# Three batches' experts issued eleven slots later in a one-core transformer kernel

## The chip, the cores and the metric

The kernel runs on one core of a Trainium2 chip. The metric is the device time of one execution in microseconds (us), the median of three runs. The core has five engines that run side by side, each working through its own queue in order: TensorE (PE, matmuls into PSUM; its weight loads are listed as PEld), VectorE (DVE), ScalarE (ACT, activation functions), GpSimd (POOL) and SyncE (SP, which here issues the DMAs). They meet only through semaphores.

## The reference

The input is four batches of 512 tokens with 128 channels. Four blocks follow each other, each added to the stream through a layer norm, `x = x + _layernorm(block(_layernorm(x)))`:

```
1  six layers of banded attention (16 heads of 8, a query sees 125 keys back and itself), each with a
   feed-forward part of 512 hidden channels and two layer norms
2  a mixer: r * ((relu(k) ** 2) @ W_v), with r and k from the token and the one before it
3  causal attention, 16 heads of 8; a gate that depends on the key's phase scales the weights
4  experts:
     pooled = x.mean(axis=1)
     h = jnp.tanh(pooled @ W1 + b1)
     probs = jax.nn.softmax(h @ W2 + b2)
     top_p, top_i = jax.lax.top_k(probs, 3)
     w = top_p / top_p.sum()
     x + sum over the three chosen e of w[e] * gelu(x @ Wa[e]) @ Wb[e]      (hidden size 512, of 8 experts)
```

Which experts a batch uses is known only when its stream has passed block 3, and the expert's weights are fetched by that number.

## The kernel before

All work is cut into units. The six banded layers of four batches are 24 units (`UNITS`), the causal attention of the four batches another four. Each unit has a fixed timetable in slots, and `whole_phase` walks through all slots `g` once for every engine: in each slot it asks small functions (`maxima_due`, `exps_due`, `late_due`, `experts_due`, ...) what is due, and issues it in the order in which the questions stand. So the program of every engine is fixed by these numbers alone, and units overlap because their timetables do: `base(u)` is 8 + 16 u for a banded unit, and 402, 422, 442, 462 for the causal attention of batch 0 to 3.

```
QP, KP = 0, 1
MAX0 = 8
EXP0 = 23
TAIL = (EXP0 + 16, EXP0 + 22)
CAT, OUT = 2, 3
ROUTE = TAIL[1] + OUT + 7
EXPERT0 = ROUTE + 5
ENDING = EXPERT0 + 2 * TOP + 1
```

For the causal attention of a batch, counted from its base: projections in slots 0 and 1; maxima of the scores in 8 to 27 (PE `causal_maxima`, L479, then DVE `maxima`, L1005); scores again, exponentials and weighted sums in 23 to 44 (PE `scores`, L511, ACT `exponent`, L802, PE `weighted`, L530); transposes of the sums at 45 (L601), of the heads at 47 (L610), the output projection at 48 (`project_out`, L622). Then comes a chain that crosses all engines: the norm of the block's output at 49 and the norm of the new stream at 52 (`statistics` on DVE, L1140 and L1144; `norm_root` on POOL, L1363 to L1370; `scale_norm` on ACT, L890; `norm_add` on POOL, L1375), transposed rows (`turn_rows` on PE, L662, `place_rows` on ACT, L898), the router at 55 (L694, L911), its logits at 56 (L702, L1187), the exponential (L916) and the choice at 57 (`route_top`, L1194 to L1201), and at 58 the loads of the three experts' weights by SP (`load_expert`, L1509 and L1511) and the spreading of their shares (L711, L1205).

The experts stand at 60, 62 and 64: `expert_hidden` (PE, L719, four chunks of 512 columns) with `expert_gelu` (ACT, L925, four gelus); two slots after each, at 62, 64 and 66, `expert_out` (PE, L730, 32 matmuls in the trace) with `add_expert` (DVE, L1210). At 67 (`ENDING`) the last norm of the batch begins, at 69 its part of the output is stored (L1547).

Three things tie the engines together there. PE writes scores and expert chunks into the same three PSUM banks (`a`), each of which must be emptied by ACT before its next use, and maxima, projections and expert outputs into four banks (`d`) that DVE empties. ACT changes its function table (ACT_TABLE_LOAD, 1.28 us in the trace) between exponentials and gelus. And the expert weights have four buffers, so that a load for job n waits until job n - 4 has been through `expert_out`.

Since the bases are 20 slots apart, batch b's experts fall into the maxima, exponentials and transposes of batch b + 1 and the first maxima of batch b + 2. Batch 0 has its experts in slots 462 to 468, batch 1 in 482 to 488, batch 2 in 502 to 508, batch 3 in 522 to 528. The output projections are in slots 450, 470, 490 and 510.

Of the kernel before, what the change touches and what calls it, by code (L numbers as in the profile page):

```python
# [6 lines left out]
BATCH, SEQ = 4, 512  # L7
# [6 lines left out]
EXPERTS, ROUTER, TOP = 8, 32, 3  # L14
# [25 lines left out]
UNITS = LAYERS * BATCH  # L40
# [30 lines left out]
TAIL = (EXP0 + 16, EXP0 + 22)  # L71
CAT, OUT = 2, 3
# [5 lines left out]
ROUTE = TAIL[1] + OUT + 7  # L78
EXPERT0 = ROUTE + 5
ENDING = EXPERT0 + 2 * TOP + 1  # L80

COL_BQ, COL_BK, COL_BV, COL_G1, COL_H1, COL_G2, COL_H2, COL_B1 = range(8)
COLS = 7 + CHUNKS
# [24 lines left out]
def base(u):  # L108
    return BASE + SLOTS * u if u < UNITS else CAUSAL0 + CSLOTS * (u - UNITS)
# [6 lines left out]
def due(g, at, late=None):  # L116

    late = at if late is None else late
    return [u for u in range(ALL) if base(u) + (late if causal(u) else at) == g]
# [50 lines left out]
def norm_slot(b, k):  # L170


    last = base(UNITS - BATCH + b) + AFTER
    late = base(UNITS + b)
    return (SLOTS * b, SLOTS * b + 2, last, last + 3, last + MIX + 3, last + MIX + 6,
            late + TAIL[1] + OUT + 1, late + TAIL[1] + OUT + 4, late + ENDING)[k]


def norms_due(g, at=0):
    return [(b, k) for k in range(9) for b in range(BATCH) if norm_slot(b, k) + at == g]  # L180


def turns_due(g):
    return [(b, k) for k in (1, 3, 5, 7) for b in range(BATCH) if norm_slot(b, k) + (3 if k == 1 else 2) == g]
# [7 lines left out]
def late_due(g, at):  # L192

    return [b for b in range(BATCH) if base(UNITS + b) + at == g]


def experts_due(g, at):
    return [(b, r) for b in range(BATCH) for r in range(TOP) if base(UNITS + b) + EXPERT0 + 2 * r + at == g]


def loads_due(g):
    return [l for l in range(2, LAYERS + 1) if base((l - 1) * BATCH) + SLOTS * BATCH - 6 == g]


TOTAL = base(ALL - 1) + ENDING + 3

# [10 lines left out]
def whole_phase(nc, env):  # L217

    D, A, N, S = Turns(4), Turns(3), Turns(), Turns()
    for g in range(TOTAL):  # L220
# [50 lines left out]
        for b, r in experts_due(g, 0):  # L271
            for f in range(CHUNKS):
                A.add("ehid", b, r, f)
        for b, r in experts_due(g, 2):
            D.add("eout", b, r)
# [5 lines left out]
    with ExitStack() as ctx:  # L281
# [125 lines left out]
        def tokens(t):  # L407
            return t.rearrange("p (i c) -> p i c", c=P)
# [12 lines left out]
        def _(pe):  # L421
# [313 lines left out]
            for g in range(TOTAL):  # L735
# [52 lines left out]
                for b, r in experts_due(g, 0):  # L788
                    expert_hidden(b, r)
# [190 lines left out]
        def _(dve):  # L980
# [275 lines left out]
            for g in range(TOTAL):  # L1256
# [32 lines left out]
                for b in range(BATCH):  # L1289
                    if g == norm_slot(b, 1) + 2:  # L1290
                        place(b)
# [166 lines left out]
        def _(sp):  # L1458
            d = env["dram"]

            def load(l):
                par = l % 2
                if l >= 2:
                    sp.wait_ge(xres_ready, 2 * BATCH * (l - 1))
                    sp.wait_ge(a_emptied, A.n("norm", BATCH * (l - 1) - 1, 1))
                sp.dma_start(wqk[:, par, :], d["wqk"][l]).then_inc(w_loaded[par], 16)
                sp.dma_start(cols[:, par, :], d["cols"][l]).then_inc(w_loaded[par], 16)
                sp.dma_start(wv[:, par, :], d["wv"][l]).then_inc(w_loaded[par], 16)
                sp.dma_start(wo[:, par, :], d["wo"][l]).then_inc(w_loaded[par], 16)
                if l < LAYERS:  # L1470
                    sp.dma_start(rowt[:, par, :, :].rearrange("p n c -> p (n c)"), d["rowt"][l]
                                 ).then_inc(w_loaded[par], 16)
                    sp.dma_start(w1[:, par, :], d["w1"][l]).then_inc(w_loaded[par], 16)
                    sp.dma_start(w2[:, par, :, :].rearrange("p f c -> p (f c)"), d["w2"][l]).then_inc(w_loaded[par], 16)
# [6 lines left out]
            def pack(u, name):  # L1481
                roles = QROLES if name == "q" else KROLES
                parts_, lo, packed = (qparts, q_lo, q_packed) if name == "q" else (kparts, k_lo, k_packed)
                if u >= BUFS:
                    sp.wait_ge(a_filled, A.n("exp", u - BUFS, PAIRS - 1, banks_of(u - BUFS) - 1))
                else:
                    sp.wait_ge(q_clean if name == "q" else k_clean, u + 1)
                sp.wait_ge(lo, u + 1)
                for r, n in enumerate(roles):
                    dest = (qpack[r:P:ROLE_STEP, u % BUFS, 1:1 + PAIRS * SEQ] if name == "q"  # L1490
                            else kpack[r:P:ROLE_STEP, u % BUFS, :, 0:HEADED])
                    sp.dma_start(dest, parts_[:, n, :]).then_inc(packed, 16)

            def load_max(u, half):
                sp.wait_ge(a_emptied, A.n("parts", u, half))
                for part in range(PARTS):
                    for h in range(2):
                        first = 1 + (2 * h + half) * 2 * SEQ
                        sp.dma_start(qpack[BODY + part:P:64, u % BUFS, first:first + 2 * SEQ],
                                     mrows[:, part * P + 64 * h:part * P + 64 * h + 64]).then_inc(max_loaded, 16)  # L1500

            def load_expert(b, r):
                n = job(b, r)
                if n >= EBUFS:
                    sp.wait_ge(d_filled, D.n("eout", (n - EBUFS) // TOP, (n - EBUFS) % TOP))
                elif n >= 2:
                    sp.wait_ge(d_filled, D.n("ffn", UNITS - 1))
                e = sp.value_load(number[0:1, b, r:r + 1], min_val=0, max_val=EXPERTS - 1)
                sp.dma_start(w1[:, (n + 2) % EBUFS, :], d["wa"][bass.ds(e, 1)].rearrange("o p c -> (o p) c")  # L1509
                             ).then_inc(e_loaded[n % EBUFS], 16)  # L1510
                sp.dma_start(w2[:, (n + 2) % EBUFS, :, :].rearrange("p f c -> p (f c)"),  # L1511
                             d["wb"][bass.ds(e, 1)].rearrange("o p c -> (o p) c")).then_inc(e_loaded[n % EBUFS], 16)
# [18 lines left out]
            for g in range(TOTAL):  # L1531
                for half in range(2):
                    for u in due(g, MAX0 + 10 + 8 * half, MAX0 + 12 + 10 * half):
                        load_max(u, half)
                for u in due(g, QP + 1):
                    pack(u, "q")
                for u in due(g, KP + 1):
                    pack(u, "k")
                for l in loads_due(g):
                    load(l)  # L1540
                for b in late_due(g, ROUTE + 3):
                    sp.wait_ge(chosen_ready, b + 1)
                    for r in range(TOP):
                        load_expert(b, r)
                for b in late_due(g, ENDING + 2):
                    sp.wait_ge(added, S.n(b, 8))
                    sp.dma_start(env["out_rows"][:, b * TILES:(b + 1) * TILES, :], tokens(stream[:, b, :])  # L1547
                                 ).then_inc(stored, 16)
# [93 lines left out]
```

## Time and profile before

| | us |
|---|---|
| median of three runs | 1324.84 (1324.23 to 1325.89) |
| the profiled execution, its own time | 1324.06 |
| its span, first to last instruction | 1322.3 |
| PE busy | 1049.7 |
| DVE busy | 801.6 |
| ACT busy | 779.2 |
| POOL busy | 404.7 |
| mean granted clock of TensorE | 0.916 of full speed |

The time of an execution is some 1.8 us longer than its span. Busy times count instructions that compute; an engine that waits for a semaphore is not busy. A row of the timeline gives the start and length in us, the engine, the line of the kernel, the operation and, in brackets, the idle time before it and what ended it. The granted clock (PEclk) is 1.00 at 2.4 GHz and 0.50 at 1.2 GHz; values in between are a mean over a stretch.

### The profile page before, as it was taken

The numbers are of one execution on the slowest core, as the hardware profiler recorded it, in microseconds if no ns is written. First come the engines' busy times: TensorE is split into PE (matmuls) and PEld (weight loads), VectorE is DVE, ScalarE is ACT, GpSimd is POOL, SyncE is SP. The second block draws the span as 40 slices with busy tenths as digits, with TensorE's granted clock in tenths as the row PEclk, the third lists the DMA queues.
The fourth block names the chain that finished last, engine by engine and source line by source line (L and its number), as shares of the span: only waits on it lengthen the run. The fifth ranks groups of instructions, "written<-read, shape, count | busy, mean of one in ns | idle before, by whom it ended". The sixth has DMA issues, their size and how long they took to land.

```text
span 1322.3 us, 46954 instructions
## 1 busy us (share of the span) xinstructions
PE 1049.7 (79%) x20080; PEld 725.7 (55%) x20080; DVE 801.6 (61%) x2451; ACT 779.2 (59%) x1419; POOL 404.7 (31%) x544
## 2 busy tenths in 40 slices
PE   1466999999999999988999899977667768887935
PEld 0245666666666666666666666655434335444513
DVE  2466667666666777775666766666477765643111
ACT  5144666666666666656666666665545757566531
POOL 4323233332323323322233333334444422202020
PEclk9578999999999999999999999989768979897957
DMA  4211212213211311131221321200201203010110
GB/s 133 48 51 51 50 52 51 52 51 87 51 37 44 85 46 46 41 85 51 51 52 51 87 52 51 52 11 16 36 14 37 42 12 97 11 50 9 49 56 9
DMA packets 72626, 64.79 MB, mean 49 GB/s; under 512 B 16226, under 2 KB 66914, under 8 KB 72418
## 3 DMA queue, kind: packets, MB, share of 16 engines
q1 hardware_dynamic: 72418, 61.78, 18.4%
q8 instruction: 159, 2.61, 0.8%
q14 instruction: 49, 0.40, 0.1%
HBM read 15.70 MB, written 1.05 MB: 13 GB/s over the span
## 4 chain that ended last, share of the span: by engine, by line
PE 46%; DVE 21%; ACT 14%; issue 8%; POOL 7%; SPq 2%; DMA 2%; POOLq 0%; ACTq 0%; DVEq 0%
DVE mx L1008 9%; PE d L647 7%; PE s L530 6%; PE a L511 5%; ACT probs L802 4%; PE d L730 3%; DVE ztok L1119 3%; PE a L637 3%; PE a L430 3%; PE d L430 3%; PE a L719 2%; PE d L557 2%; PE d L545 2%; PE d L464 2%; ACT L880 2%
## 5 line engine op out<-in xcount | busy, mean ns | idle before, releaser
L802 ACT ACTIVATE probs<-a 128x443 f32<-128x443 f32 (+2 forms) x736 | 358.3, 538 | 251.1 <-PE a L511 247.8
L1008 DVE TENSOR_REDUCE mx<-d 128x2 f32<-128x378 f32 (+1 forms) x768 | 346.4, 508 | 102.7 <-PE d L464 102.6
L530 PE MATMUL s<-probs,vals 128*32 128x189 f32 (+5 forms) x3968 | 193.1, 320 | 14.7 <-ACT probs L802 14.4
L530 PEld LDWEIGHTS s<-probs,vals 128*32 128x32 f32 x3968 | 122.9, 112 | 56.9 <-ACT probs L802 20.1
L511 PE MATMUL a<-qpack,kpack 64*64 64x189 bf16 (+4 forms) x3968 | 141.9, 242 | 0.0
L430 PE MATMUL d<-band,identb 64*64 64x252 bf16 x1152 | 89.6, 301 | 60.1 <-DVE mx L1008 44.5
L464 PE MATMUL d<-kpack,qpack 62*64 62x189 bf16 (+1 forms) x3072 | 128.2, 242 | 0.0
L1005 DVE TENSOR_REDUCE mx<-d 128x1 f32<-128x512 f32 (+7 forms) x256 | 98.3, 445 | 28.5 <-PE d L479 28.1
L1334 POOL TENSOR_SCALAR veps<-mv 128x4 f32<-128x4 f32 x48 | 11.0, 228 | 306.1 <-DVE mv L1109 306.0
L430 PE MATMUL a<-band,identb 64*64 64x252 bf16 x1152 | 83.8, 281 | 18.6 <-ACT probs L802 11.4
L637 PE MATMUL a<-xmid,w 128*128 128x512 f32 x192 | 94.4, 618 | 4.1 <-ACT hid L880 4.1
L430 PEld LDWEIGHTS d<-band,identb 64*64 64x64 bf16 x1152 | 33.2, 105 | 113.3 <-DVE mx L1008 65.6
L647 PE MATMUL d<-w,hid 128*128 128x128 f32 x768 | 92.1, 278 | 0.0
L464 PEld LDWEIGHTS d<-kpack,qpack 62*64 62x64 bf16 x3072 | 90.9, 111 | 0.7
L647 PEld LDWEIGHTS d<-w,hid 128*128 128x128 f32 x768 | 87.6, 192 | 2.9 <-issue 0.2
L1363 POOL TENSOR_SCALAR nveps<-nmv 128x4 f32<-128x4 f32 x36 | 8.3, 231 | 252.9 <-DVE nmv L1144 252.8
L511 PEld LDWEIGHTS a<-qpack,kpack 64*64 64x64 bf16 x3968 | 82.5, 110 | 0.6
L1353 POOL TENSOR_TENSOR scaled<-ztok,rowt 128x512 f32<-128x512 f32 x48 | 60.9, 1268 | 50.9 <-DVE ztok L1119 50.9
L662 PE MATMUL a<-ident,xres 128*128 128x128 f32 x64 | 15.5, 388 | 69.3 <-ACT xres L890 38.0
L545 PE MATMUL d<-state,wqk 128*128 128x512 f32 x112 | 68.7, 699 | 0.8 <-ACT state L901 0.7
L1099 DVE TENSOR_TENSOR y<-d,xres 128x512 f32<-128x512 f32 x48 | 33.2, 691 | 57.9 <-PE d L647 52.7
L637 PEld LDWEIGHTS a<-xmid,w 128*128 128x128 f32 x192 | 35.6, 196 | 58.2 <-issue 29.9
(180 smaller groups left out, 1926.4 us busy)
## 6 DMA issues: line engine op xcount, KB each, us to landing
kpack<-kparts SPq DMA_DIRECT2D x168, 128.2 KB, 2.9
qpack<-qparts SPq DMA_DIRECT2D x168, 128.0 KB, 3.2
qpack<-mrows SPq DMA_DIRECT2D x224, 4.0 KB
w<-in_w SPq DMA_DIRECT2D x12, 256.0 KB, 3.8
w<-in_wa SPq DMA_DIRECT2D x12, 256.0 KB, 3.1
w<-in_wb SPq DMA_DIRECT2D x12, 256.0 KB, 3.5
rowt<-in_rowt SPq DMA_DIRECT2D x6, 384.0 KB, 3.6
stream<-in_x SPq DMA_DIRECT2D x4, 256.0 KB, 4.9
```

The source lines that it names most:

```text
L430: pe.matmul(out, identb[rows, rows], rhs.unsqueeze(1).to_broadcast([64, 2, 2, EDGE]), start=True, stop=False, skip_group_check=True)
L464: mm = pe.matmul(banks[e][64 * h:64 * h + 64, n * width:(n + 1) * width], qpack[rows, buf, pair * SEQ + 1 + 64 * t:pair * SEQ + 65 + 64 * ...
L511: mm = pe.matmul(banks[e][64 * h:64 * h + 64, col:col + w], kpack[rows, buf, pair, own + 64 * c:own + 64 * c + 64], qpack[rows, buf, first ...
L530: mm = pe.matmul(s_ps[32 * j:32 * j + 32, q0:q0 + w - skip], vals[:, u % 2, at:at + 32], probs[:, n % SETS, j, col + skip:col + w], start= ...
L545: pe.matmul(d_ps[D.bank(name, u)][:, :], wqk[:, weights_of(u), which * P:(which + 1) * P], state[:, u % BATCH, 1:HEADED], start=True, stop ...
L637: pe.matmul(a_ps[A.bank("hid", u, f)][:, :], w1[:, weights_of(u), f * P:(f + 1) * P], xmid[:, :], start=True, stop=True).then_inc(a_filled, 1)
L647: mm = pe.matmul(bank[:, i * P:(i + 1) * P], hid[:, u % 2, f, i * P:(i + 1) * P], w2[:, weights_of(u), f, :], start=(f == 0 and i == 0), s ...
L730: mm = pe.matmul(bank[:, i * P:(i + 1) * P], hid[:, n % 2, f, i * P:(i + 1) * P], w2[:, (n + 2) % EBUFS, f, :], start=(f == 0 and i == 0), ...
L802: act.activation(probs[:, n % SETS, j, 0:width], a_ps[A.bank("exp", u, v, b)][:, 0:width], ACT.Exp, scale=SCALE).then_inc(a_emptied, 1)
L1005: red = dve.tensor_reduce(out[:, t:t + 1], bank[:, col:col + 64 * (t + 1)], AX.X, ALU.max)
L1008: red = dve.tensor_reduce(out[:, 2 * tb:2 * tb + 2], bank[:, 0:2 * width].rearrange("p (t k) -> p t k", k=width), AX.X, ALU.max)
L1353: pool.tensor_tensor(scaled[:, :, :], ztok[:, :, :], by.unsqueeze(1).to_broadcast([P, TILES, P]), ALU.mult).then_inc(scaled_ready, 1)
```

## The change

The experts of batches 0, 1 and 2 and all that follows them (last norm, store) stand eleven slots later; batch 3's stay. The loads of the weights stay where they were. New places: batch 0 in slots 473 to 479, batch 1 in 493 to 499, batch 2 in 513 to 519; last norms in 480, 500 and 520 in place of 469, 489 and 509. So a batch's experts now follow the output projection of the next batch (470, 490, 510) and lie between its two norms and its routing.

```diff
+BEHIND = 11
...
-            late + TAIL[1] + OUT + 1, late + TAIL[1] + OUT + 4, late + ENDING)[k]
+            late + TAIL[1] + OUT + 1, late + TAIL[1] + OUT + 4, late + put_off(b) + ENDING)[k]
...
+def put_off(b):
+
+    return BEHIND if b < BATCH - 1 else 0
+
+
 def experts_due(g, at):
-    return [(b, r) for b in range(BATCH) for r in range(TOP) if base(UNITS + b) + EXPERT0 + 2 * r + at == g]
+    return [(b, r) for b in range(BATCH) for r in range(TOP)
+            if base(UNITS + b) + put_off(b) + EXPERT0 + 2 * r + at == g]
+
+
+def stores_due(g):
+    return [b for b in range(BATCH) if base(UNITS + b) + put_off(b) + ENDING + 2 == g]
...
-                for b in late_due(g, ENDING + 2):
+                for b in stores_due(g):
                     sp.wait_ge(added, S.n(b, 8))
```

Lines of the changed kernel are up to eleven higher than those of the kernel before: L719 becomes L730, and L730 becomes L741.

PE at the end of the program, before: from the second half of batch 2's first expert (an `expert_hidden` is L719, an `expert_out` L730) to the spreading of batch 3's shares.

```order
L730 MATMUL d<-w,hid 128x128 x16
L530 MATMUL s<-probs,vals 32x256 x4
L719 MATMUL a<-state,w 128x512 x4
L730 MATMUL d<-w,hid 128x128 x16
L601 MATMUL d<-ident,sums 128x128 x8
L730 MATMUL d<-w,hid 128x128 x16
L610 MATMUL a<-ident,otok 128x128 x4
L622 MATMUL a<-wo,ocat 128x128 x4
L662 MATMUL a<-ident,xres 128x128 x4
L694 MATMUL a<-pooled,rw 32x1
L702 MATMUL d<-rw,hr 1x8
L711 MATMUL d<-share,ones 128x8
```

PE at the same place in the changed kernel: from the last weighted sum of batch 3 on.

```order
L541 MATMUL s<-probs,vals 32x256 x4
L612 MATMUL d<-ident,sums 128x128 x8
L621 MATMUL a<-ident,otok 128x128 x4
L633 MATMUL a<-wo,ocat 128x128 x4
L730 MATMUL a<-state,w 128x512 x8
L741 MATMUL d<-w,hid 128x128 x16
L673 MATMUL a<-ident,xres 128x128 x4
L705 MATMUL a<-pooled,rw 32x1
L730 MATMUL a<-state,w 128x512 x4
L741 MATMUL d<-w,hid 128x128 x16
L713 MATMUL d<-rw,hr 1x8
L741 MATMUL d<-w,hid 128x128 x16
```

No expert is left ahead of the transposes and the output projection of batch 3 (now L612, L621, L633). Two `expert_hidden` and one `expert_out` of batch 2 stand between that projection and the transposed rows (L673), one of each between the router (L705) and the logits (L713), and the last `expert_out` behind the logits.

ACT between the two norms of batch 2 (L890) and the placing of its rows (L898), slots 492 to 496, before: exponentials of batch 3 (L802) between them.

```order
L890 ACTIVATE normed<-xres,noffset,nrstd 128x128 x4
L802 ACTIVATE probs<-a 128x256 x4
L802 ACTIVATE probs<-a 128x512 x2
L844 COPY sums<-s 128x512
L890 ACTIVATE xres<-stream,noffset,nrstd 128x128 x4
L802 ACTIVATE probs<-a 128x512 x2
L898 ACTIVATE state,pooled<-a 128x512
```

ACT at the same place in the changed kernel, up to where the exponentials of slot 496 begin.

```order
L901 ACTIVATE normed<-xres,noffset,nrstd 128x128 x4
L813 ACTIVATE probs<-a 128x256 x2
L936 ACT_TABLE_LOAD
L936 ACTIVATE hid<-a 128x512 x4
L813 ACT_TABLE_LOAD
L813 ACTIVATE probs<-a 128x256 x2
L813 ACTIVATE probs<-a 128x512 x2
L855 COPY sums<-s 128x512
L901 ACTIVATE xres<-stream,noffset,nrstd 128x128 x4
L936 ACT_TABLE_LOAD
L936 ACTIVATE hid<-a 128x512 x4
L813 ACT_TABLE_LOAD
```

Batch 1's gelus (L936) stand now on both sides of the second norm (the second L901), each group between two table loads.

## Rows read from the trace of the kernel before

**Rows 1.** The page, part 1: busy us, share of the span, instructions.
```profile
PE 1049.7 (79%) x20080; PEld 725.7 (55%) x20080; DVE 801.6 (61%) x2451; ACT 779.2 (59%) x1419; POOL 404.7 (31%) x544
```

**Rows 2.** Busy times by stretch: PE, PEld, DVE, ACT, POOL, then PEclk, DMA share, GB/s.
```profile
1043.00:1071.00 28.00, 19.09 (x340) 11.19 (x340) 18.42 (x63) 14.95 (x33) 13.21 (x27) 0.82 0.32 59
...
1097.00:1136.00 39.00, 37.15 (x465) 23.36 (x460) 18.45 (x47) 24.41 (x40) 8.81 (x18) 1.00 0.27 77
1136.00:1165.00 29.00, 21.24 (x442) 10.84 (x446) 20.74 (x79) 20.05 (x46) 7.47 (x14) 0.76 0.09 28
1165.00:1202.00 37.00, 33.09 (x380) 20.41 (x373) 13.96 (x38) 22.57 (x36) 0.00 (x0) 1.00 0.10 32
1202.00:1229.00 27.00, 19.28 (x266) 8.23 (x260) 4.92 (x34) 19.66 (x45) 7.47 (x14) 0.63 0.14 37
1229.00:1258.00 29.00, 26.27 (x189) 17.46 (x181) 4.24 (x11) 14.35 (x23) 0.00 (x0) 0.99 0.09 32
1258.00:1282.00 24.00, 3.49 (x19) 2.70 (x20) 4.95 (x34) 8.14 (x19) 7.45 (x14) 0.55 0.14 36
```

**Rows 3.** Timeline of PE (start, us): first matmuls of slots 462, 470, 473, 481, 490, 493, 502.
```profile
1097.20 0.26 PE L435 MATMUL d<-band,identb 64*64 64x64 bf16 x8
...
1135.92 0.22 PE L435 MATMUL d<-band,identb 64*64 64x64 bf16 x4
...
1142.57 0.23 PE L435 MATMUL d<-band,identb 64*64 64x64 bf16 x8
...
1162.80 0.26 PE L435 MATMUL d<-band,identb 64*64 64x64 bf16 x8 [0.51 <-DVE mx L1005]
...
1201.75 0.26 PE L435 MATMUL a<-band,identb 64*64 64x64 bf16 x8
...
1208.26 0.22 PE L435 MATMUL a<-band,identb 64*64 64x64 bf16 x4 [0.69 <-ACT probs L802]
...
1228.81 0.32 PE L435 MATMUL a<-band,identb 64*64 64x64 bf16 x8
```

**Rows 4.** Groups by line, 1097 to 1136 (busy us, mean ns, idle before).
```profile
L719 PE MATMUL a<-state,w 128*128 128x512 f32 x24 | 11.7, 615 | 0.8 <-ACT hid L925 0.6
L730 PE MATMUL d<-w,hid 128*128 128x128 f32 x96 | 11.3, 276 | 0.0
...
L925 ACT ACTIVATE hid<-a 128x512 f32<-128x512 f32 x12 | 6.5, 597 | 0.7 <-PE a L719 0.7
...
L802 ACT ACT_TABLE_LOAD x3 | 3.8, 1283 | 7.4 <-PE a L511 7.4
...
L545 PE MATMUL d<-state,wqk 128*128 128x512 f32 x4 | 2.2, 644 | 0.0
```

**Rows 5.** Timeline of ACT, then of PE: three waits (idle before, releaser).
```profile
1058.18 0.26 ACT L831 ACTIVATE win<-g 128x64 f32<-128x64 f32 x1 [1.73 <-POOL g L1401]
...
1142.26 0.26 PE L435 MATMUL a<-band,identb 64*64 64x64 bf16 x8 [1.95 <-ACT probs L802]
...
1217.25 1.09 PE L662 MATMUL a<-ident,xres 128*128 128x128 f32 x4 [1.80 <-ACT xres L890]
```

**Rows 6.** Timeline of PE: sixteen weighted sums at either clock.
```profile
1200.16 1.07 PE L530 MATMUL s<-probs,vals 128*32 128x448 f32 x16
...
1222.96 1.93 PE L530 MATMUL s<-probs,vals 128*32 128x448 f32 x16
```

**Rows 7.** Timeline of PE and ACT, then the chain, of the last stretch.
```profile
1257.96 1.13 PE L622 MATMUL a<-wo,ocat 128*128 128x128 f32 x8 [0.96 <-ACT ocat L853]
...
1264.31 1.65 ACT L890 ACTIVATE normed<-xres,noffset,nrstd 128x128 f32<-128x128 f32 x4 [1.98 <-POOL stream L1375]
...
1270.61 1.65 ACT L890 ACTIVATE xres<-stream,noffset,nrstd 128x128 f32<-128x128 f32 x4 [4.66 <-POOL noffset L1370]
...
1278.80 2.86 DMA w<-in_wb
...
1281.70 10.01 PE L719 MATMUL a<-state,w 128*128 128x512 f32 x16 [2.93 <-DMA w<-in_wb]
```

## The prediction

> **What bounds the kernel now.** I read the page's busy times first: TensorE (PE) leads with 79%, ScalarE (ACT) and VectorE (DVE) stand near 60% [rows 1]. No engine is full, so the order decides, stretch by stretch. The busy times by stretch come next [rows 2]. Slots (g) are named as in the section on the kernel; the PE timeline says when some of them start [rows 3]. Two kinds of stretch alternate. Where a batch's experts run (1097 to 1136, 1165 to 1202, 1229 to 1258) PE is busy 37.2 of 39, 33.1 of 37 and 26.3 of 29 us at a granted clock near 1. Where the norms and the routing of the batch before its experts run (1136 to 1165, 1202 to 1229) it is busy 21.2 of 29 and 19.3 of 27 at 0.76 and 0.63, and in the last such stretch, 1258 to 1282, 3.5 of 24 [rows 2]. The change moves three batches' experts from the first kind into the second.
>
> One batch's experts cost, in 1097 to 1136 [rows 4]: PE 11.7 + 11.3 = 23.0 us, ACT 6.5 of gelus and six table loads of 1.28 (three into the gelus, three back; the row has the three back, 3.8), 14.2 together. In the last stretch, batch 3's chain is bare: the output projection starts at 1257.96, the first norm scales at 1264.31, the second at 1270.61, the weights of the first expert travel until 1281.66, and its first matmul runs at 1281.70: 23.7 us [rows 7]. Nothing on PE can hide it, since all other work is done.
>
> **The change, term by term.** No instruction of the computation is added or taken away; the order has two table loads fewer, both from batch 2.
>
> *Batch 2, taken away.* Slot 502 to the output projection is 1228.81 to 1257.96, 29.15 us [rows 3, 7]. Of PE's 26.3 busy us 23.0 are experts, of ACT's 14.35 some 6.5 + 3.8 [rows 2, 4]. What is left is a chain: 3.3 of PE, 4.0 of ACT, 1.5 of DVE, and about eight hand-overs of 0.1 to 0.2. It can't overlap itself, so I take the sum, 10.4, not the bound by PE alone, 3.3. Gain **18.7**.
>
> *Batch 2, put back into the chain.* From the start of the output projection: (a) the last norm of batch 2 no longer stands before batch 3's first scaling, which started at 1264.31, released by that add [rows 7]; its own offsets are ready 1.3 us earlier: -1.3. (b) ACT scales the second norm of batch 3 (1.65) ahead of the gelus of expert 1, and PE has to finish the fourth chunk of expert 1 (0.9, after the first gelu, 0.6) and the second half of expert 0 (11.3 / 3, about 3.6 net) before it transposes the rows of batch 3: +5.0. (c) Expert 2's first half and expert 1's second half, 3.8 + 3.6, stand before the logits' matmul: +7.2, less 0.2 of overlap and 0.6, as the exp table is now loaded while PE works. (d) Expert 2's second half lies beside routing and weight loads (2.9 for a load [rows 7]): nothing; if that cover went, 3.6. (e) The moved norm of batch 2 stands on ACT before batch 3's gelus: +0.6. Together 23.7 becomes 34.4: cost **10.7**. Both halves of (b) and (c) rest on in-order queues: what is queued behind the expert matmuls on PE is the chain itself.
>
> *Batch 0, slots 462 to 469.* They take 38.7 us, 1097.20 to 1135.92 [rows 3]. Left on PE are 37.2 - 23.0 = 14.2, on DVE 16.2 (18.45 less three adds): the floor. The nearest stretch without experts, 1043 to 1071, takes 28 with 18.4 of DVE [rows 2], but a norm stalls it too. Another cover goes: the gates of the next batch. In the nearest stretch ACT's window waited for GpSimd until 1058.18 [rows 5], 15 us into it; experts hid this. I take 20.5 (floor 16.2, ceiling 27). Gain **18.2**. In slot 470 to 472 batch 0's norm goes away; with it goes most of PE's 1.95 wait before 1142.26 [rows 5]: gain 2.2. Put back, at 473 to 480: the slots took 1142.57 to 1162.80, 20.2, unloaded [rows 3]. Loaded, I start from 38.7, take off what only 462 to 469 have (projections 2.2 [rows 4]; phase, transposes, values and gates, a like number of small matmuls, 4 by estimate) and add what only 473 to 480 have: ACT's two norm passes of 1.65 [rows 7] and the placing of the rows, 4.1, which now stand between exps and gelus, and some 4 of waits where a gelu or exp that PE needs queues behind them: 40.5. Cost **20.3**. The moved norm (DVE to GpSimd to ACT, behind slot 481's exps) costs 1.7, half of its 3.4 chain, as DVE has slack. Sum: **+1.6**.
>
> *Batch 1.* Slots 481 to 489 take 38.95, 1162.80 to 1201.75 [rows 3]; without experts PE has 10 of work and DVE 12; I take 17.3, as slot 481 alone has 1.8: gain **21.7**. Its norm in 490 goes: gain 1.5. At 493 to 501 the slots took 20.55, at low clock and with waits as the 1.80 before 1217.25 [rows 3, 5]; loaded, 38.95 + 4.1 of norm passes - 3.3 (transposes and values, and a wait for weights that 13 more slots cover) = 39.7: cost **19.2**. Moved norm: 1.5. Sum: **-2.5**.
>
> Total -8.0 - 2.5 + 1.6 = **-8.9**: 1324.06 - 8.9 = 1315.2 for an execution like the profiled one. The median of the runs is 0.8 above it, so about 1316. The moved weight loads and stores on SP and the adds on GpSimd pass queues that are idle there: the first load needs its buffer four jobs earlier, freed three slots before or more. Nothing. The uncertain terms are the two 20-us swaps, where bounds of ±3 and ±4 each remain.
>
> *A rule beside the rows.* The table load shows 1.28 us here [rows 4] and the gelu or exp follows at once. The Trainium skill (ScalarE: Activation LUTs, What ACT_TABLE_LOAD costs) budgets a drain on top, some 2.7 us a switch. By it the two loads saved would be 5.3 rather than 2.6; both lie in the 18.7, which was taken from rows, so I leave the sum.
>
> **Rivals.** *B: the idle time is filled whole.* For: in 1136 to 1165 and 1202 to 1229 PE's clock is 0.76 and 0.63, so its 21.2 and 19.3 busy us would be about 16 and 11.5 at full rate; with 23.0 added and 4 idle (as loaded stretches have 2 to 4) they take 43 and 39 in place of 29 and 27. Added 14.5 and 12 instead of 20.3 + 1.7 and 19.2 + 1.5: 13 to 16 us better than the sum if all of it came true; against: ACT, in order, has 20 + 14 and waits for offsets in between. I price it at the bulk of that: **1304**.
>
> *C: the swaps lose more.* The norm chains stand in front of exps at their full 3.4 and 2.8, and loaded slots 473 to 480 take 43: +1.7, +1.3, +2.5, and clock in emptied slots +2. It eats the gain: **1323.5**, no change.
>
> *D: the clock, slower.* PE's work in the emptied slots is 14 in 20 and 10 in 17 us, shares like 1202 to 1229, which was granted 0.63 [rows 2]. The weighted sums show both levels: 16 take 1.07 us at 2.4 GHz and 1.93 at 1.2 [rows 6]. A pair of slots then takes 4 in place of 3: 8 pairs, +8. And in the chain PE idles 4.6 us behind ACT's first norm; experts that follow run at half clock, as after 1281.70, where 16 matmuls took 10.01 in place of 7.4 [rows 7]; a second half at half clock is +3.6, two of them +7. Then -8.9 + 15 = +6: **1331**. It decides from the point at which more than 9 us of matmul time is lost. Against it: 1043 to 1071, a light stretch too, was granted 0.82 [rows 2]. The Trainium skill (TensorE: Matmul & The Clock Gate, Part 1) states that the lower clock is the default and work releases it; by that rule work spread thin over a waiting chain runs cold, and the time would be D's.
>
> *E: the change doesn't do what it says.* The order of both kernels shows the moves on PE and ACT; no chance is left to it.
>
> **Chances.** Forecast 0.50 (its own range 1309 to 1322), B 0.20, C 0.15, D 0.15. Two runs of this kernel can be told apart from about 0.2%, 2.7 us. Faster: 0.45 + 0.20 + 0.04 = 0.69; same: 0.05 + 0.09 = 0.14; slower: D's 0.15 and 0.02 of C, 0.17. The likeliest time is 1316; the range takes in B nearly whole and D in part: 1303 to 1329.
>
> **What would show it.** Right: the chain from output projection to the first matmul of batch 3's experts is 33 to 36 us instead of 23.7 and slot 502 to that projection 10 to 11 instead of 29.15; slots 462 to 469 take about 20, 473 to 480 about 40. Right for (c): the logits' matmul stands behind expert matmuls. B: loaded slots take under 37. D: clock under 0.8 in 462 to 469 and 1.93-us sums there. Wrong altogether: if the loaded slots take over 45, or if weights of batch 3 are issued late because the route result waits elsewhere than on PE.

## The result and the profile after

| | before | after |
|---|---|---|
| median of five runs, us | 1325.89 (1324.23 to 1329.45) | 1318.57 (1317.32 to 1322.06) |
| ratio, 95% interval | | 0.9942 (0.9924 to 0.9959) |
| profiled execution, us | 1324.06 | 1322.06 |
| its span, us | 1322.3 | 1320.3 |

The change makes the kernel 0.58% faster, 7.3 us by the medians. The page, part 1, of the changed kernel is to be held against [rows 1]: the work is the same, with two table loads fewer on ACT (x1417 in place of x1419).

```profile
PE 1051.0 (80%) x20080; PEld 727.7 (55%) x20080; DVE 802.1 (61%) x2451; ACT 776.0 (59%) x1417; POOL 405.0 (31%) x544
```

The two profiled executions differ by 2.0 us only. The reason lies ahead of the change: up to slot 462 the two programs are the same, yet the changed kernel's profile comes there 7.0 us later (1104.23 against 1097.20). From slot 462 to the end it takes 216.07 us where the kernel before took 225.10, that is **-9.03 us** against a forecast of -8.9. The reading by stretches below uses this part alone. First the slot starts of the changed kernel on the timeline of PE (462, 470, 473, 481, 490, 493, 502), which answer to [rows 3]:

```profile
1104.23 0.26 PE L446 MATMUL d<-band,identb 64*64 64x64 bf16 x8
...
1122.54 0.22 PE L446 MATMUL d<-band,identb 64*64 64x64 bf16 x4
...
1127.04 0.23 PE L446 MATMUL d<-band,identb 64*64 64x64 bf16 x8
...
1167.47 0.26 PE L446 MATMUL d<-band,identb 64*64 64x64 bf16 x8 [0.79 <-DVE mx L1016]
...
1185.46 0.26 PE L446 MATMUL a<-band,identb 64*64 64x64 bf16 x8
...
1190.55 0.22 PE L446 MATMUL a<-band,identb 64*64 64x64 bf16 x4 [0.69 <-ACT probs L813]
...
1229.62 0.26 PE L446 MATMUL a<-band,identb 64*64 64x64 bf16 x8
```

And the busy times of the same stretches, to be held against [rows 2] (PE, PEld, DVE, ACT, POOL, granted clock, DMA share, GB/s):

```profile
1104.20:1122.50 18.30, 16.17 (x332) 8.53 (x328) 15.75 (x44) 10.16 (x22) 8.83 (x18) 0.91 0.67 159
1127.00:1167.50 40.50, 33.04 (x382) 20.18 (x376) 15.76 (x58) 27.66 (x50) 4.58 (x9) 1.00 0.06 18
1169.30:1185.50 16.20, 12.28 (x265) 5.83 (x267) 12.48 (x36) 10.21 (x23) 2.92 (x5) 0.89 0.15 44
1190.50:1229.60 39.10, 33.70 (x306) 19.73 (x306) 6.35 (x31) 27.84 (x51) 4.11 (x9) 0.96 0.09 28
1229.60:1243.80 14.20, 7.46 (x73) 3.73 (x69) 1.56 (x4) 5.48 (x13) 2.63 (x4) 0.62 0.18 56
1243.80:1278.40 34.60, 27.02 (x138) 18.89 (x138) 7.60 (x39) 14.49 (x28) 4.98 (x11) 0.91 0.05 17
```

The reader is to see three things. The loaded stretches (second and fourth row) have PE busy 33 to 34 of some 40 us at nearly the full clock, where the routing stood alone at 0.76 and 0.63 [rows 2]. The emptied ones (first and third) are short and close to what PE or DVE have to do, 16.17 of 18.3 and 12.48 of 16.2; the third row leaves out the first 1.8 us of slot 481. And the fifth, between slot 502 and the output projection, has 7.46 us of work in 14.2 at a clock of 0.62: a stall that the forecast did not have. The timeline of PE shows it, from slot 502's second group of matmuls on, with one row of ACT at the end:

```profile
1233.32 0.27 PE L446 MATMUL a<-band,identb 64*64 64x64 bf16 x4 [3.23 <-ACT probs L813]
...
1233.80 1.93 PE L541 MATMUL s<-probs,vals 128*32 128x320 f32 x16
...
1238.79 1.94 PE L612 MATMUL d<-ident,sums 128*128 128x128 f32 x8 [0.80 <-ACT sums L855]
1241.72 1.09 PE L621 MATMUL a<-ident,otok 128*128 128x128 f32 x4 [1.00 <-DVE otok L1094]
1243.77 2.05 PE L633 MATMUL a<-wo,ocat 128*128 128x128 f32 x8 [0.96 <-ACT ocat L864]
...
1231.14 1.65 ACT L901 ACTIVATE normed<-xres,noffset,nrstd 128x128 f32<-128x128 f32 x4 [1.34 <-POOL noffset L1381]
```

ACT comes to the scaling of batch 1's moved norm (L901), finds GpSimd's offset not ready, waits 1.34 us, scales for 1.65, and only then makes the exponentials that PE wants. PE waits 3.23 us, and what follows up to the output projection runs at 1.2 GHz: 16 sums in 1.93, the projection in 2.05 against 1.13 before [rows 7].

Last, the chain behind the output projection, to be held against [rows 7]: first the busy times from the first gelus on, then the timeline of PE, then that of ACT.

```profile
1253.30:1259.50 6.20, 6.13 (x11) 2.63 (x12) 0.73 (x6) 4.79 (x11) 1.66 (x4) 0.72 0.02 4
...
1253.37 6.26 PE L730 MATMUL a<-state,w 128*128 128x512 f32 x10 [4.44 <-ACT hid L936]
...
1263.03 0.60 PE L673 MATMUL a<-ident,xres 128*128 128x128 f32 x4
...
1271.76 0.19 PE L713 MATMUL d<-rw,hr 32*1 32x8 f32 x2
...
1278.44 2.84 PE L730 MATMUL a<-state,w 128*128 128x512 f32 x6 [2.40 <-DMA w<-in_wb]
1283.44 1.26 PE L730 MATMUL a<-state,w 128*128 128x512 f32 x2 [2.17 <-ACT hid L936]
...
1249.76 1.65 ACT L901 ACTIVATE normed<-xres,noffset,nrstd 128x128 f32<-128x128 f32 x4 [3.32 <-POOL noffset L1381]
...
1272.90 0.30 ACT L927 ACTIVATE rprobs<-logits,small 1x8 f32<-1x8 f32 x1 [2.70 <-DVE small L1201]
...
1279.84 1.65 ACT L901 ACTIVATE normed<-xres,noffset,nrstd 128x128 f32<-128x128 f32 x4 [6.54 <-POOL noffset L1381]
```

The same places before, on the timeline of PE:

```profile
1272.40 1.08 PE L662 MATMUL a<-ident,xres 128*128 128x128 f32 x4 [13.31 <-ACT xres L890]
...
1274.96 0.19 PE L702 MATMUL d<-rw,hr 32*1 32x8 f32 x2 [0.43 <-ACT hr L911]
```

Output projection to batch 3's first expert is 34.67 us (1243.77 to 1278.44) in place of 23.74; PE's 13.31 us of waiting have been filled with batch 2's experts, but not wholly: it waits 4.44 for the first gelus, which stand on ACT behind batch 3's first norm, and the expert matmuls behind that wait have a granted clock of 0.72.

### The profile page after: what moved, and what is told of

Same layout as the page of the kernel before. It is cut to its first block, busy times and chain, and to the rows that moved or that the text cites. A ratio compares the mean times of both kernels' runs of the same rounds, so it can differ in the third digit from the quotient of the medians.

```text
span 1320.3 us, 46952 instructions
## 1 busy us (share of the span) xinstructions
PE 1051.0 (80%) x20080; PEld 727.7 (55%) x20080; DVE 802.1 (61%) x2451; ACT 776.0 (59%) x1417; POOL 405.0 (31%) x544
## 4 chain that ended last, share of the span: by engine, by line
PE 45%; DVE 22%; ACT 14%; issue 8%; POOL 7%; SPq 2%; DMA 1%; POOLq 0%; ACTq 0%; DVEq 0%
DVE mx L1019 9%; PE d L658 7%; PE s L541 6%; PE a L522 4%; ACT probs L813 4%; PE d L741 3%; DVE ztok L1130 3%; PE a L648 3%; PE a L441 2%; PE d L441 2%; PE d L568 2%; PE d L556 2%; PE a L730 2%; POOL nrstd L1377 2%; PE d L475 2%
## 5 line engine op out<-in xcount | busy, mean ns | idle before, releaser
L541 PE MATMUL s<-probs,vals 128*32 128x189 f32 (+5 forms) x3968 | 190.3, 317 | 15.7 <-ACT probs L813 15.4
L891 ACT ACTIVATE hid<-a,cols 128x512 f32<-128x512 f32 x96 | 61.2, 686 | 3.9 <-PE a L648 2.4
```

Source lines behind the costliest of these rows:

```text
L541: mm = pe.matmul(s_ps[32 * j:32 * j + 32, q0:q0 + w - skip], vals[:, u % 2, at:at + 32], probs[:, n % SETS, j, col + skip:col + w], start= ...
L891: act.activation(hid[:, u % 2, f, :], a_ps[A.bank("hid", u, f)][:, :], ACT.Gelu, bias=cols[:, weights_of(u), at:at + 1]).then_inc(a_emptie ...
```

## The experiments

All kernels share the program ahead of slot 462. Each profile was cut at the same instructions: (A) first projection in slot 462 (L545 before) to the output projection in 470, (B) to the one in 490, (C) to the one in 510, (D) to batch 3's first expert, (E) to the end. The ratio is to the kernel before, measured beside it on the same chip. A ratio is the better guide than a median, since the kernel before itself had medians between 1325.2 and 1328.2 us in these groups of runs.

| moved later | median us (runs) | ratio, 95% interval | A | B | C | D | E | A to E |
|---|---|---|---|---|---|---|---|---|
| nothing (before) | | | 39.1 | 65.8 | 55.2 | 23.7 | 40.6 | 224.4 |
| batches 0, 1, 2 (the change) | 1318.57 (5) | 0.9942, 0.9924 to 0.9959 | 18.7 | 62.9 | 57.3 | 34.7 | 41.9 | 215.4 |
| the change again | 1317.02 (8) | 0.9923, 0.9897 to 0.9949 | 18.3 | 64.0 | 57.3 | 34.7 | 41.9 | 216.1 |
| batch 0 | 1325.71 (10) | 1.0004, 0.9988 to 1.0020 | 19.8 | 86.2 | 53.6 | 24.5 | 40.0 | 224.1 |
| batch 1 | 1327.72 (10) | 1.0023, 1.0002 to 1.0044 | 39.1 | 46.8 | 74.3 | 23.7 | 40.6 | 224.4 |
| batch 2 | 1318.62 (10) | 0.9949, 0.9931 to 0.9967 | 39.1 | 65.9 | 34.1 | 34.2 | 40.7 | 214.0 |
| all, norm of 1 in 505 | 1312.59 (4) | 0.9907, 0.9874 to 0.9940 | 18.7 | 62.9 | 52.3 | 35.2 | 40.1 | 209.0 |
| all, batch 2 by eight | 1314.46 (4) | 0.9895, 0.9876 to 0.9914 | 18.7 | 62.9 | 57.3 | 32.3 | 40.1 | 211.3 |
| both of these | 1308.52 (5) | 0.9857, 0.9836 to 0.9878 | 18.3 | 63.2 | 52.0 | 30.9 | 40.8 | 205.2 |
| batch 2 alone, by eight | 1317.08 (4) | 0.9921, 0.9903 to 0.9939 | 39.1 | 65.6 | 35.9 | 32.5 | 39.3 | 212.3 |
| as both, scaling alone later | 1309.31 (4) | 0.9856, 0.9832 to 0.9880 | 18.7 | 62.8 | 52.3 | 30.9 | 40.0 | 204.6 |
| both, batch 0 as before | 1314.01 (4) | 0.9903, 0.9865 to 0.9941 | 39.1 | 45.3 | 52.0 | 32.4 | 40.0 | 208.8 |
| batch 2 by eight, and 0 | 1316.40 (10) | 0.9920, 0.9892 to 0.9949 | 18.3 | 86.2 | 32.4 | 30.9 | 40.5 | 208.3 |

**One batch at a time.** The first three kernels move one batch's experts and last norm by eleven slots.

```diff
-BEHIND = 11
+PUT_OFF = (11, 0, 0, 0)
...
-    return BEHIND if b < BATCH - 1 else 0
+    return PUT_OFF[b]
```

The other two have `(0, 11, 0, 0)` and `(0, 0, 11, 0)`.

Batch 0 alone:

> Only batch 0's experts (and its last norm) stand eleven slots later. Theory, the terms of the forecast as the trace of the change corrects them: emptying slots 462 to 469 gives 20.4 us, filling 473 to 480 costs 20.2, its norm leaves 470 to 472 (2.2) and costs 0.7 later, so 1.7 us faster; 462 to 470 about 18.3 us, 473 to 481 about 40.4. Rival B, batch 0 carries a third of the gain or more: 3 us faster or better. The forecast as it stood: 1.6 slower.

Measured: no difference (1.0004). A gave 19.2 us and B took 20.4; C is 1.6 less (sixteen sums that took 1.93 us before [rows 6] take 1.07 there) and D 0.8 more, and from A to E 0.3 us are left. The gain of 3 us that the rival asks for is excluded by the interval, the 1.7 of the theory just so; the forecast's 1.6 slower is inside it.

Batch 1 alone:

> Only batch 1's experts stand eleven slots later. Theory: slots 481 to 501 lose 4 us; its last norm now stands in slot 501 ahead of batch 2's experts, whose matmuls cover the wait (PE had 3.2 us of it in the change), so 3 to 5 us faster, and slot 502 to the output projection of batch 3 takes 29 to 31. Rival, batch 1's gain depends on the other two moves: within 1 us of the kernel before.

Measured: not faster (1.0023, by the interval 0.3 to 5.8 us slower; by the profile the same), a miss; the rival came. The busy times from 1145 to 1192, a stretch now without experts, and below them two waits of PE and the scaling on ACT ahead of the second, show where the expected gain went. The last row of PE is from the kernel with batches 1 and 2 moved, further down:

```profile
1145.00:1192.00 47.00, 34.08 (x669) 16.64 (x670) 30.94 (x107) 28.58 (x65) 7.47 (x14) 0.78 0.13 42
...
1179.94 0.27 PE L446 MATMUL a<-band,identb 64*64 64x64 bf16 x4 [3.69 <-DMA qpack<-mrows]
...
1238.28 1.99 PE L730 MATMUL a<-state,w 128*128 128x512 f32 x4 [2.17 <-ACT probs L813]
...
1179.31 0.22 PE L452 MATMUL a<-band,identb 64*64 64x64 bf16 x4 [3.37 <-DMA qpack<-mrows]
...
1236.10 1.65 ACT L901 ACTIVATE normed<-xres,noffset,nrstd 128x128 f32<-128x128 f32 x4 [1.35 <-POOL noffset L1381]
```

Without experts in slots 482 to 488 a transfer that they used to hide is waited for (3.69 us), so B falls by 19.0 only. Where batch 0's experts stand in the slots ahead, as in the change, the wait does not appear and B falls by 23.3 (86.2 to 62.9); without them it is there again (3.37, the added row). So what batch 1's swap gives depends on batch 0's. C grows by 19.1, most of it the moved experts themselves (18.2 where no norm stands in their way, 34.1 against 52.3); with batch 2's experts still in 502 to 508, batch 1's norm stands on ACT ahead of their gelus, and PE waits 2.17. Nothing is left.

Batch 2 alone:

> Only batch 2's experts stand eleven slots later. Theory, the 14.15 us that the change takes from slot 502 to the output projection come from the moved norm of batch 1 (ACT waits in slot 501, PE idles 3.2 us and falls to 1.2 GHz): without that norm there this stretch takes 10 to 11.5 us as forecast, the chain to batch 3's first expert matmul 34 to 35, and the kernel is 6 to 7.5 us faster. Rival, the stretch is a dependent chain that runs at the lower clock anyhow, since PE has little to do in it: 13 to 14.5 us, and the kernel is 3 to 4 us faster.

Measured: 0.9949, as much as the full change within the noise, and a chain of 34.2 us. Its timeline of PE from slot 502 to the output projection:

```profile
1228.24 0.25 PE L446 MATMUL a<-band,identb 64*64 64x64 bf16 x8
...
1233.42 1.07 PE L612 MATMUL d<-ident,sums 128*128 128x128 f32 x8 [0.80 <-ACT sums L855]
...
1237.36 1.13 PE L633 MATMUL a<-wo,ocat 128*128 128x128 f32 x8 [0.96 <-ACT ocat L864]
```

That stretch is 9.1 us (1228.24 to 1237.36) at full clock where the change takes 14.15, and batch 1's norm is the one thing that the change has there in addition. So the forecast's 10.4 was 1.3 too high for what it counted, and what it charged for the neighbour, 1.5, was 3.5 too low: the norm costs 5.0 there.

**The norm put out of the way.** Batch 1's last norm starts five slots later (505), behind the last exponentials; the experts stay.

```diff
+PUT_OFF = (11, 11, 11, 0)
+END_OFF = (11, 16, 11, 0)
...
-            late + TAIL[1] + OUT + 1, late + TAIL[1] + OUT + 4, late + put_off(b) + ENDING)[k]
+            late + TAIL[1] + OUT + 1, late + TAIL[1] + OUT + 4, late + end_off(b) + ENDING)[k]
```

> The change, with batch 1's last norm five slots later (505 in place of 500), behind the copy of the last sums, where ACT waits 4.2 us for PE and DVE. Theory, norm in the way plus clock: slot 502 to the output projection takes 10 to 11.5 us instead of 14.15, and the kernel is about 3 us faster than the change, 10 to 12 faster than the kernel before. Rival, the low clock comes from the thin work and not from the wait: only the wait of 3.2 us in slots 501 and 502 goes, the matmuls of 1.94 us (transposes of the sums) stay at half clock, 1 to 2 us gained.

Measured: 0.9907, and 5.0 us less than the change in C; the ratios are 0.35% apart, 4.6 us. Slot 502 to the output projection takes 9.1 us, less than the 10 to 11.5 expected, and no 1.94 is left, against the rival. PE, then ACT:

```profile
1226.92 1.07 PE L547 MATMUL s<-probs,vals 128*32 128x320 f32 x16 [0.15 <-ACT probs L819]
...
1230.45 1.07 PE L618 MATMUL d<-ident,sums 128*128 128x128 f32 x8 [0.80 <-ACT sums L861]
...
1234.39 1.13 PE L639 MATMUL a<-wo,ocat 128*128 128x128 f32 x8 [0.96 <-ACT ocat L870]
...
1229.72 0.59 ACT L861 COPY sums<-s 128x512 f32<-128x512 f32 x1 [0.76 <-PE s L547]
1230.20 1.65 ACT L907 ACTIVATE normed<-xres,noffset,nrstd 128x128 f32<-128x128 f32 x4
```

The same scaling, 1.65 us long, follows the copy of the sums without a wait and nobody waits for it. Of the 5.0 us, 2.5 are the wait (3.23 less the 0.7 that PE waits at that place anyway) and 2.6 the clock: 1.93 - 1.07, 1.94 - 1.07, 1.09 - 0.63 and 1.08 - 0.64 for the sums and transposes. The wait and the low clock came together in all three profiles of kernels that scale this norm in slot 501 with batch 2's experts moved, and neither is in the sums and the transposes of the sums of the four that scale it five slots later, nor of the three that move batch 2 but not batch 1. The output projection is no such sign: it took 2.05 us also in two kernels without the wait (batch 2 alone by eight, and batches 1 and 2), and 1.13 in the other five. The intervals of 0.9907 and of the change overlap a little; the same step shows again below, between both moves together and all three with batch 2 by eight (5.3 in C, 0.9857 against 0.9895).

**Batch 2 by eight slots.** Its experts stand in 510, 512 and 514 in place of 513, 515 and 517; its norm stays in 520.

```diff
+PUT_OFF = (11, 11, 8, 0)
+END_OFF = (11, 11, 11, 0)
```

> The change, but batch 2's experts stand eight slots later instead of eleven (slots 510, 512, 514, last output in 516; its last norm stays in 520). Theory (the time that batch 2's experts cost in the projection chain is set by where their hidden matmuls meet ScalarE: in the change the first hidden half stands behind batch 3's first norm scaling and TensorE waits 4.44 us for ACT's gelu; in slot 510 it stands ahead of it): the stretch from the output projection in slot 510 to batch 3's first expert falls from 34.7 us to 31 to 32 us, and batch 2's last norm is done before batch 3's first gelu is wanted, which takes away up to 2.2 us more. In all 3 to 6 us below the change: 1312.5 to 1315.5 us. Rival (TensorE's work is the same and the chain merely idles elsewhere, at the wait on the router's answer): no difference beyond 1 us, 1317.5 to 1319.5.

Measured: 0.9895, and 4.1 us below the change from A to E; by the ratios it is 0.3 to 0.5% ahead. D falls by 2.4, E by 1.8. The busy times of the first expert matmuls behind the wait, then PE and ACT at that place:

```profile
1246.60:1251.70 5.10, 4.89 (x13) 2.13 (x13) 0.00 (x0) 4.62 (x12) 1.70 (x3) 1.00 0.00 0
...
1246.69 4.95 PE L736 MATMUL a<-state,w 128*128 128x512 f32 x10 [0.31 <-ACT hid L942]
...
1273.54 9.51 PE L736 MATMUL a<-state,w 128*128 128x512 f32 x16 [3.13 <-DMA w<-in_wb]
...
1246.04 1.57 ACT L942 ACTIVATE hid<-a 128x512 f32<-128x512 f32 x3
...
1248.35 1.64 ACT L907 ACTIVATE normed<-xres,noffset,nrstd 128x128 f32<-128x128 f32 x4
```

The gelus now fill the time in which ACT waited 3.32 us for the offset, PE's wait of 4.44 is 0.31, the ten matmuls behind it take 4.95 us at full clock where the change took 6.26, and the 2.17 ahead of batch 3's later expert matmuls is gone. The same work on the same engines, three slots apart.

**Both together**, and both with batches 0 and 1 as before:

> Both moves together: batch 2's experts in slots 510, 512, 514, and batch 1's last norm in slot 505 instead of 500. The two places lie 20 us apart and share no wait. Theory: the gains add (5 to 6 us from the norm, 3 to 6 us from the slots), 1307 to 1311 us, the stretch from slot 502 to the projection of slot 510 about 9 to 10 us as with the norm alone. Rival (the norm in 505 stands in the way of batch 2's routing or of the experts in slot 510, so that the gains don't add): 1312 to 1314 us.

> Batches 0 and 1 as before, batch 2's experts alone in slots 510, 512, 514. Theory (batches 0 and 1 each give and take about the same; batch 2 is what pays): batch 2 alone in its old form measured 6.7 us below before; with the better slots 3 to 6 us more, 1312 to 1316 us, that is 3 to 6 us above the kernel that moves all three and batch 1's norm. Rival (batches 0 and 1 are worth nothing even together): the same as that kernel within 1.5 us.

Measured: 0.9857 for both together, the gains add. With batch 2 alone 0.9921, more than was expected between the two, and the intervals are apart: moving batches 0 and 1 is worth some 8.5 us (0.0064 of 1326, 4.8 to 12.2 from the two intervals) when batch 1's norm is out of the way. The profiles have 7.1 us between them, of which up to 3.4 can be the clock in C (see below). Of the 8.5, 5.0 are the norm (0.9857 against 0.9895). With the norm in the way 3.4 are left by eight slots (0.9895 against 0.9921, the intervals overlap), and 1 to 3 by eleven (0.9942 and 0.9923 against 0.9949): nothing that stands clear of the noise.

**Scaling later, statistics not.** The statistics of the norm stay in slots 480 and 500; only ACT's scaling and GpSimd's addition come four and five slots later, for batch 0 too.

```diff
+END_OFF = (11, 11, 11, 0)
+LAG = (4, 5, 0, 0)
...
+            if norm_slot(b, k) + at + (LAG[b] if k == 8 else 0) == g]
```

> Batch 2's experts in slots 510, 512, 514; the last norms of batches 0 and 1 keep their statistics in slots 480 and 500, but their scaling and addition come 4 and 5 slots later. Theory (TensorE waits 2.28 us after slot 481 and 3.2 us in slot 501 because ACT stands in order behind the norm's scaling, which waits for GpSimd's offset): both waits go, the one in slot 501 with its fall to the lower clock, so 5 to 8 us below the same kernel without the lag, and 0 to 2 us below the one that moves batch 1's norm whole. Rival (the work of VectorE and GpSimd for the statistics delays batch 2's routing as much): as the kernel without the lag within 1 us.

Measured: 0.9856, the same as both together. The wait in slot 501 went, as expected, but the one after slot 481, which was to go too, only moved. PE's row without the lag, then PE and ACT with it:

```profile
1170.56 0.27 PE L452 MATMUL a<-band,identb 64*64 64x64 bf16 x4 [2.28 <-ACT probs L819]
```

```profile
1175.78 0.26 PE L459 MATMUL a<-band,identb 64*64 64x64 bf16 x8 [2.09 <-ACT probs L826]
...
1173.59 1.65 ACT L914 ACTIVATE normed<-xres,noffset,nrstd 128x128 f32<-128x128 f32 x4
```

ACT no longer waits for GpSimd, but the 1.65 us of scaling themselves stand between exponentials at this place too.

**Which of batches 0 and 1.** Both together less batch 0, and batch 2 by eight with batch 0 alone:

> Batch 0's experts as before, batches 1 and 2 in the better form (batch 1 eleven slots later with its norm in slot 505, batch 2 in slots 510, 512, 514). The open point: the kernel that moves all three measured 7.1 us less from slot 462 to the end (205.2) than the one that moves batch 2 alone (212.3), though batch 0 alone measured 0.3 and batch 1 alone 0. Theory (batch 1's swap pays only where batch 0's experts stand in slots 473 to 480: without them slots 482 to 489 give 19.0 us, with them 23.3, and slots 493 to 501 take 18.2 with the norm out of the way): 19.0 less 18.2, so 1 us below batch 2 alone, about 211.5 us from slot 462 to the end. Rival (the gain lies in batch 1 with its norm out of the way, and batch 0 adds nothing): 205 to 207 us.

> Batch 1's experts as before, batch 0's eleven slots later, batch 2's in slots 510, 512, 514. Theory (the gain of 7.1 us needs batch 1; batch 0 alone gives and takes the same): 212 us from slot 462 to the end, as with batch 2 alone (212.3), within 0.5. Rival (the gain lies in batch 0's swap): 205 to 209 us.

Measured: 0.9903 and 0.9920. For the first, A to E came out at 208.8, between the two expectations (211.5, and 205 to 207), and its time lies between its neighbours with overlapping intervals: how the 8.5 us divide stays open. The second had 208.3, 4.0 below batch 2 alone by eight, inside the rival's range, which looks like a gain from batch 0; the times of the runs show none (0.9920 against 0.9921, each within 0.2 to 0.3%). The profiles tell where the 4.0 are: 3.4 of them in C, where the two kernels have the same work in the same order. Busy times and sums in slots 499 to 501 of batch 2 alone by eight, then with batch 0:

```profile
1225.30:1233.40 8.10, 7.10 (x98) 2.86 (x98) 1.54 (x11) 4.73 (x12) 0.00 (x0) 0.52 0.47 146
...
1230.19 1.93 PE L547 MATMUL s<-probs,vals 128*32 128x384 f32 x16
```

```profile
1226.20:1231.90 5.70, 4.20 (x98) 1.97 (x98) 1.81 (x12) 4.87 (x12) 0.00 (x0) 1.00 0.28 81
...
1229.75 1.07 PE L547 MATMUL s<-probs,vals 128*32 128x384 f32 x16
```

The same 98 matmuls take 7.10 us at a granted clock of 0.52 and 4.20 at 1.00; in the 3 us before, both had 0.50. Whether this belongs to the execution or to the kernel the runs leave open. The sixteen sums of slot 499 took 1.07 us in both profiles with batch 0 moved and batch 1 not (1227.07 and 1227.09), and 1.93 in all three with both in their old places (before, batch 2 by eleven, by eight); yet the timed runs show no gain from it. So one profile can credit an edit with some 3 us of clock that the median does not give.

**The change again**, for the noise:

> The change itself once more, in the same job, for the noise of the segments and of the time. Theory: from slot 462 to the end 215.4 us within 0.5 in a second profile, while the part ahead of slot 462, whose program all these kernels share, differs by some us from profile to profile (1097.9 to 1105.8 so far); median 1317 to 1320 us. Rival (the segments differ as much as the part ahead): 212 to 219 us.

Measured: median 1317.02; 216.1 from A to E in place of 215.4, 0.2 outside the band that was given, C, D and E the same within 0.1, A 0.4 less, B 1.1 more. The 1.1 can be seen. In both profiles PE waits 2.3 us for ACT behind slot 481, and the sixteen sums behind that wait are, in the first and in the second:

```profile
1173.87 1.07 PE L541 MATMUL s<-probs,vals 128*32 128x320 f32 x16
```

```profile
1174.74 1.93 PE L541 MATMUL s<-probs,vals 128*32 128x320 f32 x16
```

One program, the same wait, and the clock fell in one execution and not in the other. The same wait stands in three other kernels, and the clock fell behind it in one of them (1.94 in both moves together, 1.07 in the two others). The part ahead of slot 462, the same program in all thirteen profiles, ended between 1097.9 and 1106.2.

## Why the prediction was right, and where it was not

The time (1318.57 for 1316) and the total of the part that the change touches (-9.03 for -8.9) are right. Step by step the total is a sum of errors that cancel: 3.8 us better than forecast up to slot 501, 2.2 worse from there to the projection, 0.9 worse in the chain and 0.7 behind it. That it comes within 0.2 us is luck; that the loaded slots and the chain came within 1 us each is not.

- *Slots 462 to 469*: 18.31 us for 20.5. The cover of the gates did go (ACT's window waited 2.70 us for GpSimd at 1117.11), but PE came within 2.2 us of what it has to do. *470 to 472*: gain 2.15 for 2.2.
- *Slots 473 to 480*: 40.43 for 40.5. The waits behind ACT that the forecast put at some 4 are there.
- *Slots 481 to 489* with batch 0's norm: 17.99 for 17.3 + 1.7. *490 to 492*: gain 1.42 for 1.5. *493 to 501*: 39.07 for 39.7. Slots 462 to 501 without batch 1's norm came to -6.2 for -2.4, better by 3.8.
- *Slot 502 to the projection*: 14.15 for 10.4. This is **the term that failed**. It was worked out as a chain of its own work, and that was near (9.1 with batch 2 moved alone). "*Moved norm: 1.5*" was charged to batch 1 as half of a chain with slack, but on ACT it stands ahead of exponentials that the chain itself wants: 2.5 of wait. And the half clock that rival D had for light stretches came here, 2.6 more. The norm cost 5.0 in place of 1.5, the chain 1.3 less than forecast, so the loss is 2.2 beyond the forecast.
- *The chain*: 34.67 for 33.8, which is the 34.4 less (e). (a) and (b), projection to the transposed rows: 19.26 against 14.44, +4.8 for +3.7. Of this some 1.3 is the clock: behind the wait of 4.44 ten expert matmuls took 6.26 us, and 4.95 at full clock with batch 2 by eight. (c), rows to logits: 8.73 against 2.56, +6.2 for +7.0. The 0.6 for the table load did not come: logits to first expert is 6.68 against 6.74, since the exponential waits for DVE until 1.14 us behind the logits, about as long as the load took. (d): the last `expert_out` lies wholly beside routing and the weights' travel, as forecast. (e) was 1.3 for 0.6: the moved norm of batch 2 holds up the first gelus of batch 3, PE waits 2.17.
- *Slips in the working*: in (c) 3.8 + 3.6 is 7.4 and not 7.2, so that the overlap of 0.2 was taken off twice; rival B's 19.3 busy us at 0.63 are 12.2 at full rate and not 11.5; and the weight loads, which the working calls moved, stay where they were. None moves the sum by more than 0.2.

Rival B (idle time filled whole) did not come: the loaded slots took 40.4 and 39.1, not under 37. Of D two places came true in part: 1229.6 to 1243.8 at 0.62 (2.6 us), and the experts in the chain behind ACT's first norm, where PE waited 4.44 us as D had it (4.6) and lost 1.3, not 7. But the clock in 462 to 469 was 0.91, not under 0.8, and in 481 to 489 0.89, and the whole loss is far from the 9 us from which D decides. The rule of the Trainium skill named with D (TensorE: Matmul & The Clock Gate, Part 1) states that the lower clock is the default and work releases it; the trace agrees at this place, where the sums behind 3.23 us without work ran at 1.2 GHz, but the time that D drew from it did not come.

How the gain divides was right in outline. The terms said batch 2 gives 8.0 and batches 0 and 1 together 0.9. Batch 2 alone does give the whole (0.9949), and 0 and 1 nothing that shows in the form of the change. What was not seen is that this hangs on where batch 1's norm stands: with the norm five slots later moving both is worth some 8.5 us (4.8 to 12.2). The best kernels, both moves together and the one with the later scaling, are 1.4% faster than the kernel before (0.9857 and 0.9856) and some 9 to 11 us ahead of the change by the ratios.

## What to carry to other kernels

When work is moved, list what moves with it (here a norm of 1.65 us on ACT) and read, on the engine where it lands, which instruction stands right behind it and who waits for that; a scaling of 1.65 us ahead of a needed exponential cost 5 us here with the clock that fell behind it, and five slots later nothing. Put filler work where an in-order engine waits for something else, and put it ahead of the instruction that waits. Compare kernels by timed runs, and use a single profile to explain a difference, not to prove one of a few us.

## What the hardware showed that was not expected

- The part ahead of slot 462, one program in all these kernels, ended between 1097.9 and 1106.2 us in thirteen profiles. An edit's effect is read better from the part that it touches, cut at the same instructions, than from the span of one profile.
- The granted clock is not fixed by the program alone. In two profiles of the change sixteen sums behind a wait of 2.3 us took 1.07 us in one and 1.93 in the other. And 98 matmuls in the same order, in two kernels that differ in batch 0 alone, ran at 0.52 in one profile and at 1.00 in the other, 7.10 against 4.20 us busy; in the second PE had even waited longer just before, 2.26 us against 1.80 for the transposed rows, so the length of that wait does not explain it. Why they differ stays open.
- Behind a wait of 3.2 us in slot 501, by contrast, the low clock was there for the sums, the transposes and the output projection in all three profiles that have it. Three profiles are few, and the runs give no rule for when it falls.
